# Self-attention of layers 0 and 2: the order of batch 1's own chain against group 0's maxima, and TensorE products whose result nobody reads

## What is computed

```
x = x + cross_attention(layernorm(x), ctx)         # softmax over 77 keys, 16 or 8 heads
h = layernorm(x); n = layernorm(h) (layer 0) or rmsnorm(h) (layer 2)
q, k, v = n @ Wq, n @ Wk, n @ Wv                   # 16 heads of 8
att = softmax(q k^T / sqrt(8))                     # 512 x 512 for each of 2 batches x 16 heads
h = h + (att v) @ Wo ; x = x + h + experts(norm(h))
```

## Time and profile before

| | us |
|---|---|
| median of 3 runs | 1214.75 |
| range | 1213.97 to 1216.38 |
| the profiled execution | 1213.29 |
| its span | 1211.2 |
| TensorE matmul busy | 950.1 (78%) |
| VectorE busy | 561.1 (46%) |
| ScalarE busy | 440.2 (36%) |
| GpSimd busy | 242.0 (20%) |

### The profile page before, as it was taken

One profiled execution on the slowest core, in us unless ns is written; L12 is line 12 of the kernel. 1 busy time (PEld: TensorE's weight loads), 2 busy tenths in 40 slices (PEclk: granted clock), 3 DMA queues, 4 the chain that ended last, 5 costly groups with the idle time before them and its releaser, 6 DMA issues. The chain is left out here.

```text
span 1211.2 us, 15544 instructions
## 1 busy us (share of the span) xinstructions
PE 950.1 (78%) x5561; PEld 648.8 (54%) x5561; DVE 561.1 (46%) x1292; ACT 440.2 (36%) x769; POOL 242.0 (20%) x283
## 2 busy tenths in 40 slices
PE   5886789634737539999768757998699979869998
PEld 3564345324635335777637742232366677747776
DVE  4784456341237363111666846774254546631111
ACT  2332355412323113343353323776322233424443
POOL 0435211032053100000374343001000012430110
PEclk9998699956978759999797976999799988978999
DMA  7005210103620000110000052210010101200111
GB/s 321 1 1 141 92 47 22 36 18 104 184 74 1 1 0 18 36 35 18 1 1 1 2 122 87 55 27 2 1 38 29 58 14 59 70 1 18 35 35 36
DMA packets 33263, 55.71 MB, mean 46 GB/s; under 512 B 3696, under 2 KB 25397, under 8 KB 32816
## 3 DMA queue, kind: packets, MB, share of 16 engines
q1 hardware_dynamic: 32176, 52.88, 14.3%
q0 software_dynamic: 1024, 1.98, 0.6%
HBM read 44.81 MB, written 9.96 MB: 45 GB/s over the span
## 5 line engine op out<-in xcount | busy, mean ns | idle before, releaser
L2269 PE MATMUL psum<-xT_all,wexp 128*128 128x512 f32 x400 | 184.0, 605 | 1.3 <-issue 0.7
L1483 DVE TENSOR_REDUCE arena<-psum 128x2 f32<-128x1024 f32 (+3 forms) x128 | 127.7, 1021 | 71.5 <-PE psum L2057 43.5
L1038 ACT ACTIVATE arena<-psum 128x512 f32<-128x512 f32 (+3 forms) x256 | 115.9, 515 | 78.3 <-PE psum L2070 40.1
L732 POOL TENSOR_TENSOR rstd<-var,held 128x4 f32<-128x4 f32 (+3 forms) x30 | 54.4, 1826 | 403.0 <-DVE var L1241 385.9
L2269 PEld LDWEIGHTS psum<-xT_all,wexp 128*128 128x128 f32 x400 | 74.4, 196 | 78.3 <-issue 72.6
L1975 PE MATMUL psum<-values_out_all,arena 128*128 128x128 f32 x560 | 80.5, 294 | 35.6 <-ACT arena L1005 26.3
L2284 PEld LDWEIGHTS psum<-wexp,arena 128*128 128x128 f32 x800 | 94.2, 192 | 16.1 <-issue 14.3
L2054 PE MATMUL psum<-arena 72*128 72x512 bf16 (+3 forms) x256 | 80.1, 384 | 27.2 <-DVE arena L1483 12.9
L798 POOL TENSOR_TENSOR arena<-arena,small 128x616 f32<-128x616 f32 x56 | 67.9, 1216 | 147.0 <-DVE small L1424 146.9
L2284 PE MATMUL psum<-wexp,arena 128*128 128x128 f32 x800 | 94.7, 275 | 0.9 <-DVE r_res L1746 0.9
L1975 PEld LDWEIGHTS psum<-values_out_all,arena 128*128 128x128 f32 x560 | 71.1, 202 | 43.7 <-ACT arena L1005 33.6
(11 more groups left out here) (282 smaller groups left out, 1439.3 us busy)
## 6 DMA issues: line engine op xcount, KB each, us to landing
wexp<-experts SPq DMA_DIRECT2D x32, 514.0 KB, 3.5
parts_k<-wexp SPq DMA_DIRECT2D x12, 384.0 KB, 2.8
arena<-parts_k SPq DMA_DIRECT2D x48, 96.0 KB
arena<-parts_q SPq DMA_DIRECT2D x48, 96.0 KB
arena<-experts SPq DMA_DIRECT2D x8, 514.0 KB, 3.8
wexp<-experts SPq DMA_DIRECT2D x9, 384.0 KB, 3.1
held<-packed SPq DMA_DIRECT2D x1, 2375.0 KB, 15.3
held<-packed SPq DMA_DIRECT2D x1, 2264.5 KB, 20.4
```

The costliest lines, as they stand in the source:

```text
L732: pool.tensor_tensor(dst, src, half[0:src.shape[0], 0:n], ALU.pow).then_inc(done, 1)
L1038: act.activation(p_self[:, n % 2, kt % 2, j, lo:S], bank(t_bank("keys", c, k), lo, S), ACT.Exp, scale=DS ** -0.5).then_inc(ut_ok, 1)
L1483: dve.tensor_reduce(top[:, x % 2, qt, j:j + 2], src, AX_X, ALU.max, negate=True).then_inc(us_ok, 1)
L2269: mm(bank(c, 0, BANK), wexp[:, side, c * P:(c + 1) * P], xT_all[:, b * S:(b + 1) * S], start=True, stop=True).then_inc(h_ps, 1)
```

## The change

SyncE and GpSimd: batch 1's parts move behind group 1's maxima, its inverse deviations and `v1` behind group 0's, and the constant rows into the cross-attention's seventh half.

```diff
+        def own_at(tick, *what):
+
+            return tick == {"tokens": 1, "k": 2, "q": 2, "v": 3}[what[0]]
...
+            for what_ in ("tokens", "k", "q"):
+                if own_at(tick_, what_):
+                    t_place["own", what_] = len(t_place)
+            if own_at(tick_, "v"):
+                s_place["own", "v"] = len(s_place)
...
@@ -656,17 +665,19 @@
                 split_stored(sp, u, 0)
                 for x in range(4):
                     load_group(u, x)
-                store_split(u, 1)
-                split_stored(sp, u, 1)
-                for side in range(2):
-                    if u == 0:
-                        load0(side, side)
-                    else:
-                        load(2, side, side)
                 for x in range(GROUPS):
                     load_top(u, x)
+                    if x == 1:
+                        store_split(u, 1)
+                        split_stored(sp, u, 1)
                     if 1 <= x < 5:
                         load_group(u, x + 3)
+                    if x == 1:
+                        for side in range(2):
+                            if u == 0:
+                                load0(side, side)
+                            else:
+                                load(2, side, side)
...
@@ -742,7 +753,10 @@
             def split_keys(u, b):
 
                 at = B * u + b + 1
-                pool.wait_ge(hi_ok, 2 * at - 1)
+                if b == 0:
+                    pool.wait_ge(hi_ok, 2 * at - 1)
+                else:
+                    pool.wait_ge(ut_ok, t_count(u, "own", "k"))
...
@@ -777,17 +794,16 @@
                         rsqrt(rstd[:, n % 4, :], var[:, n % 4, :], qvar_ok, n + 1, qrstd_ok)
                 u = l // 2 if l in (0, 2) else None
                 if u is not None:
-                    pool.wait_ge(x_xTp, 2 * l + 2)
-                    if l == 2:
-                        pool.wait_ge(qrstd_ok, NT)
-                    pool.memset(U["k"][64:96, :], ONES_IN_PAIRS).then_inc(ones_set, 1)
-                    pool.wait_ge(ones_set, u + 1)
                     pool.wait_ge(vw_ps, FIRST_W[l] + 4)
                 pool.memset(E4[l][:, :, HALF:CHUNKED], 0.0).then_inc(pads_ok, 1)
                 for n in range(HALVES[l]):
                     at = FIRST_HALF[l] + n
                     if u is not None and n == 3:
                         pool.memset(U["v0"], 1.0).then_inc(wide_set, 1)
+                    if u is not None and n == 6:
+                        pool.wait_ge(e_mul, at)
+                        pool.memset(U["k"][64:96, :], ONES_IN_PAIRS).then_inc(ones_set, 1)
+                        pool.wait_ge(ones_set, u + 1)
...
@@ -805,13 +821,6 @@
                 l = 2 * u
                 split_keys(u, 0)
                 split_queries(u, 0)
-                batch_tokens(1, a_stat, SELF_AT[l] + 2, a_rstd)
-                batch_tokens(1, b_stat, B * u + 2, b_rstd)
-                pool.wait_ge(pT_ps, FIRST_HALF[l] + HALVES[l])
-                pool.memset(U["v1"], 1.0).then_inc(wide_set, 1)
-                split_keys(u, 1)
-                split_queries(u, 1)
-
...
+                    if x == 0:
+                        batch_tokens(1, a_stat, SELF_AT[l] + 2, a_rstd)
+                        batch_tokens(1, b_stat, B * u + 2, b_rstd)
+                        pool.wait_ge(pT_ps, FIRST_HALF[l] + HALVES[l])
+                        pool.memset(U["v1"], 1.0).then_inc(wide_set, 1)
+                    if x == 1:
...
+                        split_keys(u, 1)
+                        split_queries(u, 1)
                 batch_tokens(1, m_stat, MOE_AT[l] + 2, m_rstd)
 
             def queues():
@@ -1007,28 +1024,31 @@
```

```diff
-                        last = dve.tensor_tensor(heads_of(keys[:, b * 2 * HALF:(b + 1) * 2 * HALF]),
-                                                 bank(0, b * KV, (b + 1) * KV).unsqueeze(1).broadcast_to([P, HS, KV]),
-                                                 w("headmask").unsqueeze(2).broadcast_to([P, HS, KV]), ALU.mult)
-                    last.then_inc(k_own, 1)
+                        dve.tensor_tensor(heads_of(keys[:, b * 2 * HALF:(b + 1) * 2 * HALF]),
+                                          bank(7, b * KV, (b + 1) * KV).unsqueeze(1).broadcast_to([P, HS, KV]),
+                                          w("headmask").unsqueeze(2).broadcast_to([P, HS, KV]), ALU.mult).then_inc(k_own, 1)
                     return
...
+                                                 bank(6, b * KV, (b + 1) * KV).unsqueeze(1).broadcast_to([P, HS, KV]),
                                                  w("headmask").unsqueeze(2).broadcast_to([P, HS, KV]), ALU.mult)
                     last.then_inc(v_own, 1)
...
                 if l == 0:
                     own_keys(l)
+                    own_values(l)
                 dve.wait_ge(x_rstd, l + 1)
...
-                elif l != 1:
+                elif l == 3:
                     own_values(l)
+                if l in (0, 3):
                     values_through(l)
...
-                self_moments(u, 1)
-                self_residual(u, 1)
-                self_normal(u, 1)
...
                 for tick in MOMENTS:
-                    if tick == 7 - LEAD:
-                        self_values(u, 1, 4)
...
+                    if a == 7:
+                        self_moments(u, 1)
+                    if a == 9:
+                        self_residual(u, 1)
+                    if a == 11:
+                        self_normal(u, 1)
+                    if own_at(tick, "v"):
+                        self_values(u, 1, s_bank("own", "v"))
...
                     for g in range(G):
-                        last = mm(bank(g // 3, g % 3 * 154, g % 3 * 154 + 154), wk[:, g * P:(g + 1) * P], cT,
+                        last = mm(bank((0 if l else 7) + g // 3, g % 3 * 154, g % 3 * 154 + 154), wk[:, g * P:(g + 1) * P], cT,
                                   start=True, stop=True)
                     last.then_inc(k_ps, 1)
                 for g in range(G):
-                    last = mm(bank((4 if l == 2 else 3) + g // 3, g % 3 * 154, g % 3 * 154 + 154), wv[:, g * P:(g + 1) * P], cT,
+                    last = mm(bank([6, 3, 4, 3][l] + g // 3, g % 3 * 154, g % 3 * 154 + 154), wv[:, g * P:(g + 1) * P], cT,
                               start=True, stop=True)
...
-                    pe.wait_ge(k_own, l + 1)
+                    if l:
+                        pe.wait_ge(k_own, l + 2)
                     for b, half in parts:
-                        if entry == 1:
+                        if l == 0:
+                            pe.wait_ge(k_own, b + 1)
+                        elif entry == 1:
                             pe.wait_ge(v_own, l + 1)
...
                 else:
                     for t in range(TB):
                         last = mm(bank(n, t * P, (t + 1) * P), xT_self[:, t * P:(t + 1) * P], wn, start=True, stop=True)
-                last.then_inc(pj_ps, 1)
...
-                pe.wait_ge(v_in_ok, B * u + 1)
+                pe.wait_ge(v_in_ok, u + 1)
...
-                    elif kt == 0:
+                    if n == 4 * TB:
+                        pe.wait_ge(us_ok, s_count(u, "own", "v"))
+                    if n and kt == 0:
...
+                def keep_busy(n):
+
+                    for _ in range(n):
+                        mm(bank(7, 0, P), ident_bf[:, :], later_bf[:, :], start=True, stop=True)
+
+                keep_busy(40)
                 for tick in MOMENTS:
-                    if tick == 3 - LEAD:
-                        self_turned(u, 1, 4)
-                    if tick == 4 - LEAD:
-                        self_projected(u, 1, 0, 5)
-                        self_projected(u, 1, 1, 6)
-                    if tick == 5 - LEAD:
-                        self_projected(u, 1, 2, 4)
-                    if tick == 8 - LEAD:
-                        pe.wait_ge(hi_ok, 2 * B * (u + 1))
-                        pe.wait_ge(v_in_ok, B * (u + 1))
+                    if tick < 0:
+                        keep_busy(6)
...
+                        if x == 0:
+                            pe.wait_ge(x_done, 2 + NT * (l + 1))
                         turn_top(x)
...
+                    if own_at(tick, "tokens"):
+                        t_free("own", "tokens")
+                        self_turned(u, 1, t_bank("own", "tokens"))
+                    for which, what in enumerate("kq"):
+                        if own_at(tick, what):
+                            t_free("own", what)
+                            self_projected(u, 1, which, t_bank("own", what))
+                    if own_at(tick, "v"):
+                        s_free("own", "v")
+                        self_projected(u, 1, 2, s_bank("own", "v"))
```

More of the change, by code:

```diff
@@ L754, in split_queries @@
                 at = B * u + b + 1
-                pool.wait_ge(hi_ok, 2 * at)
+                if b == 0:
+                    pool.wait_ge(hi_ok, 2 * at)
+                else:
```

(23 more changed lines are left out.)

42 lines of the change are left out of this document (22 added, 20 removed).

## The result

The changed kernel takes 1207.45 us (median of 20 runs, 1199.32 to 1215.71) against 1214.7 (20 runs, 1212.49 to 1220.19). The ratio is 0.9934 with an interval of 0.9914 to 0.9955: some 8 us faster, where 21.4 were forecast (1193.3, range 1185 to 1204). The profiled execution is the slowest of the 20, 1215.71 us with a span of 1213.8, so its end says little. What it says is where the lead goes stage by stage. A second profile of the same kernel (e12_after_again, span 1207.4) is used beside it.

The account below looks back on a forecast made before the run. No engine bounds the whole span; each stretch is held by one chain, with TensorE at half speed in places. The terms 6.6 + 10.6 + 4.2 = 21.4 us gave 1193.3 us for the median, range 1185 to 1204.

Parts of the forecast that it names:

- Part 1: First cross-attention: TensorE's waits for masked keys and values go, GpSimd's constant leaves the path; 6.6 us, bounds 3.5 to 8.
- second rival: The first cross-attention's gain is given back in the loop of halves: 1199.9 us, chance 0.10.
- Part 2: Layer 0's self-attention, maxima first: second turn at 133.4 against 142.17, 1.8 us more to the third; 10.6 us, bounds 5 to 12.
- first rival: The clock falls in both self-attentions in spite of the idle products, costing 8 us: 1201.3 us, chance 0.25.
- Group 4 can't be late: Layer 0's self-attention: group 4's data is in time, as pair 32 comes over 22 us after the second turn.
- Part 3: Layer 2's self-attention, maxima first: second turn at 748.1 against 752.31; 4.2 us, bounds 1 to 8.
- The idle products, cost: Both self-attentions: the 40 fit a 5.52 us DMA wait, six per tick run beside maxima; nothing, bounds 0 to 27 us.
- fourth rival: The idle products themselves slow the kernel, at up to 26.9 us for both stages: 1220 us, chance 0.02.
- The rule and the row: Rule: activity releases the throttle, so idle products keep the clock; trace row: 14.82 of 15.30 us busy left it at 0.51.

Follow-up runs that it names:

- e12_after_again: The changed kernel run and profiled again with nothing altered, on the same chip as the repeat of e7_held_front: 1205.84 us, ratio 0.9926.
- e1_front: Kernel before with only the first cross-attention's changes (own banks for keys and values, GpSimd's constant behind the seventh half): 1207.41 us, ratio 0.993.
- e7_held_front: e2_loads with 104 (layer 0) and 84 (layer 2) in place of 40 idle products ahead of the first scores: 1194.07 us, ratio 0.9816; repeated 1192.75 us, 0.9825.
- e15_held_ticks: e7_held_front with 26 in place of six idle products in two ticks of layer 2, while the first top row is under way: 1191.03 us, ratio 0.9802.
- e2_loads: Changed kernel with the first two expert loads behind the store of the third top row instead of ahead of it: 1195.89 us, ratio 0.9847.
- e3_noidle: Changed kernel without any idle product, neither the 40 ahead of the scores nor the six in each tick: 1206.08 us, ratio 0.9912.
- e5_loads_noidle: e2_loads without any idle product: 1195.93 us, ratio 0.9823.
- e9_collide: Kernel before with the first two expert loads moved right ahead of the third top row's DMAs, in both self-attentions: 1216.05 us, ratio 1.0009.
- e10_front_idle: e7_held_front without the six idle products in each tick: 1200.79 us, ratio 0.9886.

## Why the prediction was wrong, step by step

**Part 1, right.** Forecast 6.6 us: the first chain at 28.70 (forecast 28.8), scores 5.28 us earlier (5.2), the constant hidden. e1_front alone measured 8 us with 6 to 12 possible; its trace ends 6.6 us earlier than before's. The second rival, that the start's gain is given back, did not come.

**Part 2, the mechanism right, the clock wrong.** From first scores to the second turn I forecast 24.3 us (109.11 to 133.4). The changed kernel needed 29.5 and 28.4. This is the first rival (chance 0.25), down to its size: 3.6 plus 1 us, measured 4.1 to 5.2. What the text missed was in its own working: it put 40 idle products of 2.4 us into a wait of 5.52, called the cost nothing and took their yield for granted, though 3 us of the wait were left empty. e7_held_front, which fills it, needs 23.9, and its third turn at 35.7 answers to the forecast 36.2. The sum of Part 2 was correct for a clock that the change as made did not hold; that it agrees to half a microsecond is in part luck, since e7_held_front too has 3.5 us at half speed and e15_held_ticks, with the same layer 0, needs 26.6. One time in it does not follow from its terms: 116.7 plus 6.2 plus 2.2 is 125.1, not 125.9.

**Part 2, the step that failed.** The prediction said that "Group 4 can't be late", and that was true: no profile has TensorE waiting for group 4's data at pair 32. It did not cost what now stands in SyncE's queue ahead of the third top row: batch 1's stores and the expert loads, both moved behind the second top row, and group 4's load, which is in its old place in the program but now waits for those stores. The part on the moved DMAs of SyncE is missing, so that they were put at nothing without a reason. This is the larger term: 7.3 us in the profile from third to fourth turn (3.85 of them the wait), and 10.6 us between changed and e2_loads. The working had what it takes to see it: the third turn 10.6 us earlier brings the third row's store up to batch 1's stores (7.4 us of splits and "some 8" of transfer, both reckoned there), behind which the rest was queued. No rival held it.

**Part 3, the mechanism right, the size not.** Forecast 4.2 us at the second turn; measured 2.0 in the changed kernel (33.8 to 31.8), 3.2 in e7_held_front, 6.7 in e15_held_ticks. What is missing is again clock: first turned maxima at 13.9 in place of 12.5, with VectorE waiting behind idle products at half speed (12.1 in e3_noidle, without them). Where the clock is held to the second turn the gain is 6.7, 2.5 more than the 4.2 forecast for just that case.

**The idle products, cost.** "Nothing" holds within 2 us a layer (changed against e3_noidle, first and second turns). The fourth rival (1220) did not come.

**The rule and the row.** The rule of the Trainium skill, "TensorE: Matmul & The Clock Gate", Part 1, that activity releases the throttle, was the one I leaned to. That it holds "whatever the matmuls are" was my reading; the sentence quoted names no kind, and no run here varied the kind. My ground for leaning to it was a misreading of the earlier trace rows. The stretch that stood at 0.51 does not hold products of 75 rows alone: 30 of its 80 are bf16 products of 128 rows of the same two constant tiles as the idle ones, as the kernel before shows in this stretch:

```profile
134.12 0.31 PE L2070 MATMUL psum<-ident_bf,later_bf 128*128 128x128 bf16 x1
...
134.55 0.32 PE L2057 MATMUL psum<-later_bf,ident_bf 128*128 128x128 bf16 x1
```

So that the idle products "have all 128 rows, which the scores have not" did not set them apart. In the changed kernel 9.88 of 11.50 us busy, idle products among it, went with 0.75, and 9.30 of 9.30 with 0.50, while 10.27 of 14.50 in e7_held_front stayed at 1.00. What the engine did before differs: a gap of 3.66 us ahead of the first, none ahead of the last. That idle products can keep a clock that is already up is borne out by e7_held_front's first window and by e15_held_ticks's in layer 2; that dense work always brings a fallen clock back soon is not: the 9.30 us were dense throughout and stayed at 0.50.

**The sum.** Between 1193.3 and 1207.45 lie 14.2 us: 10.6 the backlog ahead of the third top row (changed to e2_loads), and of the other 3.6 most would be the clock (e2_loads to e7_held_front, 0.9847 to 0.9816 and 0.9825, 2.7 to 3.8 us). The first share is shown by intervals that do not touch, with idle products and without. The second rests on the traces alone: these intervals overlap, and e5_loads_noidle reaches 0.9823 without any idle product. What stays open is the spread of the changed kernel, 16 us over its runs: the runs list mean clocks of 0.875 to 0.897, and the two profiles differ in where the clock falls in stretches of equal work (814.30 on), but no experiment moved such a fall at will.

## What to carry to other kernels

When a step is moved earlier, lay the whole queue of the engine that issues its transfers beside the new times: a small transfer on the critical path must not stand behind bulk loads that have all the time in the world, and two of those that are harmless singly can be dear together. A clock that is to be kept by idle work must be kept through the whole wait; filling half of it yielded nothing here that could be told, and even the whole filling is not told in the total from leaving the idle work out, so run that kernel beside it. Measure the parts of such a change one by one: here one part gave all the gain, the other two cancelled (layer 0 lost what layer 2 gained), and moving two loads by one row turned 8 us into 19.

## What the hardware showed that I had not expected

The third top row, four DMAs of 3 KB, was in use 4.4 us after the start of its issue behind 1.03 MB of expert loads (e9_collide) and 4.05 us behind 0.58 MB in six DMAs (e2_loads), but 6 to 7.7 us behind both. When six 128-column products stood ahead of it, TensorE's next product started 0.64 us later at half clock (103.32 to 103.96 in the changed kernel) and 0.34 at full (102.31 to 102.65 in e7_held_front), so the same filler that is hidden behind a maximum of 0.41 us at one clock is not at the other. And the wait of 3.85 us for a DMA was followed by 13.10 us at 0.50 although TensorE was busy 13.05 of them: from third to fourth turn 7.3 us were lost against the kernel before, nearly twice the wait. Waits of 0.57 and 1.18 us (e9_collide, e2_loads) were not followed by such a stretch at the same place; one of 1.35 us (e10_front_idle) was.
